# Handing the result rows of routed experts back: scattered by row index or combined on TensorE, with the expert registers read earlier and the residual held in PSUM

## The chip, the cores and the metric

The kernel runs on one core of a Trainium2 chip, in one launch. The metric is the device time of a launch in microseconds (us). In the text and rows, PE is TensorE's matmuls, PEld its weight loads, DVE is VectorE, ACT is ScalarE, POOL is GpSimd and SP is SyncE. All data is float32; matmuls take it either whole (two records for each matmul) or as float32r.

## What is computed

Two layers on x of 2 x 256 tokens with 256 columns: a cross-attention with 16 heads over 512 context rows, and a mixture of experts (32 routed, 4 for each token, one shared), each behind a layer norm and with its residual. The change touches only what follows the attention's last heads.

```python
x = x + _L0_xattn_ref(_layernorm(x, axis=-1), ctx_512, ...)
x = x + _L0_ffn_ref(_layernorm(x, axis=-1), ...)
...
topk_idx, topk_w = _noaux_tc_gate(x, gate_weight, e_score_correction_bias)
combine = jnp.zeros((T, E), x.dtype).at[jnp.arange(T)[:, None], topk_idx].add(topk_w)
def body(acc, packed):
    w1e, w3e, w2e, ce = packed
    return (acc + ce[:, None] * _swiglu(x, w1e, w3e, w2e), None)
routed, _ = lax.scan(body, jnp.zeros_like(x), (w1, w3, w2, combine.T))
shared = _swiglu(x, ws1, ws3, ws2)
return (routed + shared).reshape(b, s, h)
```

T is 512 tokens (four tiles of 128, `TT`), D is 256, E is 32, the hidden width 128.

## The kernel before

Every engine has its own program in `build`, written out by hand in the order in which it runs; semaphores join them. No scheduler is at work.

**End of the attention.** `PLAN` says after which of the 64 score tiles TensorE does which step; `O` steps add a head pair's output projection to `o_ps` (banks 0 and 1). After the last, DVE adds `o_ps` to `x_sb` (L877), takes the statistics and writes the normalised rows `xn`; SP stores them to `xn_rows` in DRAM. TensorE transposes them (`rows_T`) and computes the gate's logits and the shared expert's first layer.

**Routing.** `route`, `slots`, `tables`, `top_weights` and `places` run on DVE. Each expert owns a unit of 128 rows: 64 for the first tokens of that expert and 64 for an overflow block, which may belong to another expert. TensorE turns one-hots into `idx` (L619), a table of the token of each row of each unit, and sums a count into `eo`, the expert of each overflow block. `place` says at which row of `y_rows` a token's four results will lie.

**Registers.** The overflow block's weights are found by a register. L627 reads `eo` with four loads of eight registers and checks each value against its limits. This stands behind the tables and ahead of the unit loop; then TensorE waits for `sh_sum`, DVE's adding of the shared expert (`sy_ps`) to `x_sb` (L1028).

**The unit loop.** POOL gathers a unit's 128 rows (`gather`, L1085) with six buffers: gather u waits until `x_rows(u - 6)` is done. In iteration j TensorE does `x_rows(j)` (transposes, L543), `g_rows(j - 3)` (L561), `hidden(j - 1)` (L552) and `out_rows(j - 3)` (L568). ACT evicts the transposed rows (L747) and does SiLU (L753). DVE multiplies (L1001), evicts the transposed product (L1007) and the result (L1013); SP stores the result to `y_rows` (four buffers, `yu`). Transposed products and results each alternate between two PSUM banks.

**Collection.** When all stores have landed, POOL fetches each token's four result rows, 16 indirect DMAs (`collect`, L1090) of 128 rows; DVE weighs and adds them to `x_sb` (L1041), and SP stores the output.

## Time and profile before

| | us |
|---|---|
| median of 3 runs (362.36 to 362.75) | 362.63 |
| the profiled execution | 362.5 |
| its span, first to last instruction | 360.7 |
| PE / PEld busy in the span | 279.5 / 200.3 |
| DVE / ACT / POOL busy | 230.8 / 171.3 / 138.9 |
| mean granted TensorE clock | 0.914 of 2.4 GHz |

The span is what the trace shows; the profiled execution took 1.8 us more than it. Shares of busy time are an average over a stage that TensorE and DVE share (the attention, to about 227 us), a routing stage where DVE works in short steps, the unit loop (265 to 332 us) where TensorE is busy without a gap, and the collection. The chain of waits, read in order of time, says which engine each moment hangs on; "issue" in it is time for which the profile shows no reason.

### The profile page before, as it was taken

Reading aid. Unit: us, or ns where it says so; the run is one execution under the profiler, and the core shown is the slowest. Engines: PE = TensorE matmul, PEld = TensorE weight load, DVE = VectorE, ACT = ScalarE, POOL = GpSimd, SP = SyncE. Lnnn points to the kernel's source line nnn. Section 1 sums busy time; section 2 is a strip of 40 time slices with the busy share of each in tenths; the row PEclk is TensorE's granted clock in tenths of the full one; section 3 lists DMA queues with packets and bytes.
Section 4 is the critical chain, followed back from the end, with each engine's and each line's share of the span. In section 5 each row is a group of like instructions: output and inputs, shape, how many; then the busy total and the mean of one; then the engine's idle time right before and its main releaser. Section 6 shows DMA issues by size and latency. Waiting matters only on the chain.

```text
span 360.7 us, 5449 instructions
## 1 busy us (share of the span) xinstructions
PE 279.5 (77%) x1662; PEld 200.3 (56%) x1662; DVE 230.8 (64%) x578; ACT 171.3 (47%) x400; POOL 138.9 (39%) x126
## 2 busy tenths in 40 slices
PE   3857869898899998989989898487159999996000
PEld 3634538776587765877758787355125555553000
DVE  4294853889877898968987788668604444443134
ACT  3343745767677786777865565420013333331000
POOL 0641912985009690086910000000544544500672
PEclk9998998999999999999999999968759999999555
DMA  7910015000240001500009957100123444422242
GB/s 253 410 41 0 3 44 190 2 0 0 86 149 3 1 2 26 193 2 0 2 7 351 405 200 253 61 8 1 54 64 105 143 135 139 141 74 85 77 133 85
DMA packets 17595, 35.41 MB, mean 98 GB/s; under 512 B 2848, under 2 KB 10272, under 8 KB 17568
## 3 DMA queue, kind: packets, MB, share of 16 engines
q1 hardware_dynamic: 15264, 28.77, 22.5%
q0 software_dynamic: 2304, 6.29, 6.0%
q8 instruction: 15, 0.25, 0.3%
q14 instruction: 12, 0.10, 0.1%
HBM read 29.81 MB, written 5.24 MB: 97 GB/s over the span
## 4 chain that ended last, share of the span: by engine, by line
PE 48%; DVE 20%; issue 7%; ACT 6%; POOL 4%; DMA 1%; POOLq 0%; ACTq 0%; DVEq 0%
PE bank L552 10%; PE bank L503 6%; PE bank L488 5%; PE bank L568 4%; DVE nmax L828 4%; POOL ctT L1090 4%; PE bank L543 3%; PE bank L465 3%; DVE pT L841 3%; PE bank L443 2%; PE bank L480 2%; PE bank L479 2%; PE bank L413 2%; PE bank L390 2%; PE bank L391 2%
## 5 line engine op out<-in xcount | busy, mean ns | idle before, releaser
L1085 POOL DMA_INDIRECT rope<-xn_rows,idx x32 | 30.4, 951 | 103.5 <-DVE idx L995 74.1
L303 POOL TENSOR_TENSOR rtmp<-abuf,rope 128x512 f32<-128x512 f32 x22 | 29.2, 1325 | 76.9 <-issue 59.6
L828 DVE TENSOR_REDUCE nmax<-bank 128x1 f32<-128x512 f32 x64 | 43.4, 681 | 16.5 <-PE bank L480 15.5
L698 ACT ACTIVATE prob<-bank,nmax 128x512 f32<-128x512 f32 x48 | 33.0, 689 | 30.9 <-DVE nmax L828 30.3
L841 DVE TENSOR_TENSOR pT<-bank,pT 128x512 fp32r<-128x512 f32 x64 | 43.5, 680 | 1.0 <-ACT pT L706 1.0
L706 ACT CAST pT<-bank 128x512 fp32r<-128x512 f32 x64 | 37.6, 590 | 5.6 <-PE bank L488 5.1
L503 PE MATMUL bank<-pT,kvs 128*128 128x256 f32 x256 | 39.0, 296 | 0.6 <-DVE pT L841 0.5
L1001 DVE TENSOR_TENSOR kv<-bank,kv 128x128 f32<-128x128 f32 x32 | 9.3, 291 | 43.3 <-issue 32.7
L552 PE MATMUL bank<-wall,nmat 128*64 (+1 forms) x256 | 36.5, 408 | 0.2 <-ACT nmat L747 0.2
L503 PEld LDWEIGHTS bank<-pT,kvs 128*128 128x128 f32 x256 | 33.1, 193 | 2.0 <-issue 1.0
L488 PE MATMUL bank<-ident,prob 128*128 128x128 f32 x192 | 29.4, 277 | 6.1 <-DVE pT L841 5.4
L488 PEld LDWEIGHTS bank<-ident,prob 128*128 128x128 f32 x192 | 23.0, 142 | 17.6 <-DVE prob L836 9.9
L836 DVE TENSOR_SCALAR prob<-prob,rsum 128x512 f32<-128x512 f32 x48 | 32.5, 677 | 0.1
L747 ACT COPY nmat<-bank 128x256 f32<-128x256 f32 x32 | 11.9, 372 | 39.1 <-PE bank L543 39.1
L306 POOL TENSOR_TENSOR roped<-rtmp 128x512 f32<-128x512 f32 x22 | 29.6, 1347 | 1.7
L304 POOL TENSOR_TENSOR rtmp<-abuf,rope 128x512 f32<-128x512 f32 x22 | 30.3, 1377 | 0.0
L443 PE MATMUL bank<-roped,gmat 128*128 128x512 f32 x48 | 25.4, 638 | 6.1 <-DVE msplit L794 2.8
L479 PE MATMUL bank<-kdup,qsp 128*128 128x512 f32 x64 | 28.1, 439 | 0.8 <-ACT prob L698 0.8
L480 PE MATMUL bank<-kdup,qsp 128*128 128x512 f32 x64 | 25.5, 398 | 0.0
L413 PE MATMUL bank<-wring 128*128 128x192 f32 x64 | 16.6, 400 | 10.8 <-DMA wring<-in_w_attn 4.9
L1090 POOL DMA_INDIRECT ctT<-y_rows,place x16 | 15.1, 946 | 24.2 <-DMA y_rows<-nmat 19.6
L390 PE MATMUL bank<-xnT,msplit 128*128 128x512 f32 x48 | 21.9, 456 | 3.0 <-DVE msplit L794 1.6
(169 smaller groups left out, 527.7 us busy)
## 6 DMA issues: line engine op xcount, KB each, us to landing
wall<-in_w_exp SPq DMA_DIRECT2D x32, 384.0 KB, 7.1
y_rows<-nmat SPq DMA_DIRECT2D x32, 128.0 KB, 1.7
wring<-in_w_attn SPq DMA_DIRECT2D x16, 224.0 KB, 4.1
wring<-in_w_attn SPq DMA_DIRECT2D x4, 640.0 KB, 8.1
wring<-in_w_attn SPq DMA_DIRECT2D x4, 512.0 KB, 7.0
rope<-in_rope_q SPq DMA_DIRECT2D x1, 768.0 KB, 6.7
x_sb<-in_x SPq DMA_DIRECT2D x1, 512.0 KB, 3.5
xn_rows<-xn SPq DMA_DIRECT2D x4, 128.0 KB, 1.8
```

The lines of the kernel that those rows point to most:

```text
L443: mm = pe.matmul(work[u % 2][:, :], gmat[:, j, i, :], roped[:, j, i, :], start=(i == 0), stop=(i == NQT - 1))
L479: pe.matmul(s_ps[t % 3][:, :], q, kdup[:, 0, b * L:(b + 1) * L], start=True, stop=False)
L480: pe.matmul(s_ps[t % 3][:, :], q, kdup[:, 1, b * L:(b + 1) * L], start=False, stop=True) \
L488: mm = pe.transpose(t_ps[t % 2][:, lc * P:(lc + 1) * P], probs[t % 4][:, lc * P:(lc + 1) * P], ident[:, :])
L503: mm = pe.matmul(pv_of(hb), kvs[:, b * LC + lc, :], pT[:, hl, hb % 2, lc, :], start=(n == 0), stop=(n == 2 * LC - 1))
L552: mm = pe.matmul(hu_ps[u % 2][s * BLK:(s + 1) * BLK, 0:2 * I], xTu[:, u % XS, dc, s * BLK:(s + 1) * BLK], wall[:, bass.ds(w + dc * 2 * I, ...
L698: act.activation(probs[t % 4], s_ps[t % 3][:, :], ACT.Exp, bias=nmax[:, t:t + 1], accum_out=psum_e[:, t:t + 1]).then_inc(s_exp, 1)
L706: act.copy(pT[:, 0, hb % 2, :, (t % 2) * P:(t % 2 + 1) * P], t_ps[t % 2][:, :].rearrange("p (c q) -> p c q", c=LC)).then_inc(t_hi, 1)
L828: dve.tensor_reduce(nmax[:, t:t + 1], s_ps[t % 3][:, :], AX.X, ALU.max, negate=True).then_inc(s_max, 1)
L836: dve.tensor_scalar(probs[t % 4], probs[t % 4], rsum[:, t:t + 1], None, ALU.mult).then_inc(s_norm, 1)
L841: dve.tensor_tensor(pT[:, 1, hb % 2, :, q], t_ps[t % 2][:, :].rearrange("p (c q) -> p c q", c=LC), f(pT[:, 0, hb % 2, :, q]), ALU.subtract ...
L1085: pool.indirect_dma_start(xg[:, u % XG, :], None, xn_dram, bass.IndirectOffsetOnAxis(idx[:, 1, u:u + 1], 0)) \
```

## The change

**Units in two kinds.** Twenty units are SENT: ACT evicts the result times the row's weight (`wslot`), and POOL scatters its 128 rows (`scatter`) to `y_rows`, which is now laid out by rank and token; rows without a token go to a region behind. Twelve are DIRECT (4, 9, 14, 19 and 24 to 31): ACT writes the weighted result as float32r (`y_hi`), DVE the rest (`y_lo`), DVE compares the unit's token indices with an iota row (`choose`), and TensorE adds one-hot times result into `sy_ps`, the shared expert's accumulators, eight float32r matmuls a unit (`combine`). A token's ranks that no scatter wrote have to read as zero, so SP fills 2 MB of `y_rows` with zeros early on. The collection is four plain loads on SP of a token's four ranks, summed on DVE in iterations j = 31 to 34 (`sum_rows`); the last four additions take `sy_ps`.

**Weights by slot.** `places` goes; `slot_weights` makes two more one-hot tables on DVE, and TensorE turns them into `wslot` at j = 1.

**Banks.** Transposed products have one bank and results have one (5), since bank 2 and now 7 hold `sy_ps`.

**Registers.** They are read before the tables, without the limit checks, and `eo` is made earlier in `slots`. `d_ws`, the weights' semaphore, is waited for ahead of the loop.

**x in PSUM.** Step `S0` at tile 62 adds x to `o_ps` by an identity matmul. Statistics and normalisation read PSUM; ACT copies the sum to `x_sb` beside the gate. The addition of the shared expert before the loop goes.

```diff
+DIRECT = (4, 9, 14, 19) + tuple(range(24, NU))
+SENT = tuple(u for u in range(NU) if u not in DIRECT)
+SUMS = {28: 0, 29: 1, 30: 2, 31: 3}
...
-        yu_ps = (bank[2], bank[5])
+        gt_ps = bank[6]
+        yu_ps = bank[5]
...
-            {0: "-N0", 1: "-N1", 3: "O0 O1", 5: "O2 O3", 8: "O4", 10: "O5", 12: "O6"},
+            {0: "-N0", 1: "-N1", 3: "O0 O1", 5: "O2 O3", 8: "O4", 10: "O5", 12: "O6", 14: "S0"},
...
+            sp.wait_ge(zero_set, 1)
+            sp.dma_start(y_dram[0:TOPK * T, :].rearrange("(p a r) d -> p a (r d)", p=P, a=TOPK * T * D // (P * T)),
+                         ctT[:, NP - 1, :].unsqueeze(1).to_broadcast([P, TOPK * T * D // (P * T), T])).then_inc(d_zero, 16)
...
-            for u in range(NU):
-                sp.wait_ge(yu_ev, u + 1)
-                sp.dma_start(y_dram[u * P:(u + 1) * P, :], yu[:, u % YS, :]).then_inc(d_yu[u % YS], 16)
+            for r in range(YS):
+                sp.wait_ge(d_yu[r], 16 * len(SENT[r::YS]))
+            for tt in range(TT):
+                sp.dma_start(y4[:, tt, :, :], y_dram[0:TOPK * T, :].rearrange("(k t p) d -> t p k d", k=TOPK, t=TT)[tt]) \
+                    .then_inc(d_y4[tt], 16)
...
+                elif kind == "S":
+                    for tt in range(TT):
+                        pe.matmul(o_ps[tt // 2][:, (tt % 2) * D:(tt % 2 + 1) * D], ident[:, :], x_sb[:, tt, :],
+                                  start=False, stop=False, skip_group_check=True)
...
+                if u >= 1 and u - 1 in SENT:
+                    pe.wait_ge(yu_ev, SENT.index(u - 1) + 1)
+                elif u >= 1:
+                    pe.wait_ge(y_low, DIRECT.index(u - 1) + 1)
                 for s, w in enumerate((over_w[u], u * WE)):
-                    pe.matmul(yu_ps[u % 2][s * BLK:(s + 1) * BLK, 0:D], gTu[:, u % GS, s * BLK:(s + 1) * BLK],
+                    pe.matmul(yu_ps[s * BLK:(s + 1) * BLK, 0:D], gTu[:, u % GS, s * BLK:(s + 1) * BLK],
                               wall[:, bass.ds(w + 2 * ND * I, D)], start=True, stop=True).then_inc(yu_mm, 1)
+
+            def combine(u):
+                n = DIRECT.index(u)
+                pe.wait_ge(picked, n + 1)
+                pe.wait_ge(y_low, n + 1)
+                for tt in range(TT):
+                    for k, part in enumerate((y_hi, y_lo)):
+                        mm = pe.matmul(sy_ps[tt // 2][:, (tt % 2) * D:(tt % 2 + 1) * D], pickc[:, n % 2, tt * P:(tt + 1) * P],
+                                       part[:, n % 2, :], start=False, stop=(u == DIRECT[-1] and k == 1), skip_group_check=True)
+                    if tt % 2 == 1 and (u == DIRECT[-1] or tt == TT - 1):
+                        mm.then_inc(comb_mm, 1)
...
+            pe.wait_ge(eo_done, 1)
+            over_w = []
+            for u in range(0, NU, 8):
+                _, regs = nc.values_load_multi_w_load_instructions(
+                    eo[0:1, u:u + 8], [mybir.EngineType.PE], min_val=0, max_val=(E - 1) * WE,
+                    skip_runtime_bounds_check_because="VectorE takes the minimum with the last expert just before")
+                over_w.extend(regs)
...
             pe.wait_ge(d_ws, 16 * E)
-            pe.wait_ge(eo_done, 1)
-            over_w = []
-            for u in range(0, NU, 8):
-                _, regs = nc.values_load_multi_w_load_instructions(eo[0:1, u:u + 8], [mybir.EngineType.PE], min_val=0,
-                                                                   max_val=(E - 1) * WE)
-                over_w.extend(regs)
-            pe.wait_ge(sh_sum, TT)
-            for j in range(NU + 3):
+            for j in range(NU + 4):
                 if j < NU:
                     x_rows(j)
-                if j >= 3:
+                if 3 <= j < NU + 3:
                     g_rows(j - 3)
+                if j - 4 in DIRECT:
+                    combine(j - 4)
                 if 1 <= j <= NU:
                     hidden(j - 1)
-                if j >= 3:
+                if 3 <= j < NU + 3:
                     out_rows(j - 3)
+                if j == 1:
+                    pe.wait_ge(one_w_done, 1)
+                    for k in range(NK):
+                        for s in range(2):
+                            mm = pe.matmul(invw_ps[s * BLK:(s + 1) * BLK, :], one_r[:, k, :],
+                                           one_w[:, s * T + k * E:s * T + (k + 1) * E], start=(k == 0), stop=(k == NK - 1))
+                            if k == NK - 1:
+                                mm.then_inc(invw_mm, 1)
...
+            def y_evict(u):
+                act.wait_ge(yu_mm, 2 * u + 2)
+                if u in SENT:
+                    n = SENT.index(u)
+                    if n >= YS:
+                        act.wait_ge(d_yu[n % YS], 16 * (n // YS))
+                    act.activation(yu[:, n % YS, :], yu_ps[:, 0:D], ACT.Copy, scale=wslot[:, u:u + 1]).then_inc(yu_ev, 1)
+                else:
+                    n = DIRECT.index(u)
+                    if n >= 2:
+                        act.wait_ge(comb_mm, n - 1)
+                    act.activation(y_hi[:, n % 2, :], yu_ps[:, 0:D], ACT.Copy, scale=wslot[:, u:u + 1]).then_inc(y_top, 1)
+
+            for j in range(NU + 3):
                 if j < NU:
                     x_evict(j)
-                if j >= 1:
+                if 1 <= j <= NU:
                     silu(j - 1)
+                if j == 3:
+                    act.wait_ge(w_done, 1)
+                if j >= 3:
+                    y_evict(j - 3)
...
-                dve.tensor_tensor(x_sb[:, tt, :], o_ps[tt // 2][:, (tt % 2) * D:(tt % 2 + 1) * D], x_sb[:, tt, :],
-                                  ALU.add).then_inc(x1_done, 1)
-                if tt >= 1:
-                    dve.wait_ge(x1_done, tt)
-                    dve.bn_stats(stat[:, TT + tt - 1, :], x_sb[:, tt - 1, :]).then_inc(x1_stat, 1)
-            dve.wait_ge(x1_done, TT)
-            dve.bn_stats(stat[:, 2 * TT - 1, :], x_sb[:, TT - 1, :]).then_inc(x1_stat, 1)
+                dve.bn_stats(stat[:, TT + tt, :], x1(tt)).then_inc(x1_stat, 1)
...
+            def slot_weights():
+
+                top = topw[:, 1, :, :].rearrange("p t k -> p (t k)")
+                link(dve.scalar_tensor_tensor(wvals[:, :], pick[:, :], 4096.0, top, ALU.is_ge, ALU.mult))
+                dve.tensor_tensor(one_w[:, 0:T].rearrange("p (i e) -> p i e", e=E), sel_a.rearrange("p (i e) -> p i e", e=E),
+                                  top.unsqueeze(2).to_broadcast([P, NK, E]), ALU.mult)
+                dve.tensor_tensor(one_w[:, T:2 * T].rearrange("p (i e) -> p i e", e=E), eq_v.rearrange("p (i e) -> p i e", e=E),
+                                  wvals[:, :].unsqueeze(2).to_broadcast([P, NK, E]), ALU.mult).then_inc(one_w_done, 1)
+                dve.wait_ge(invw_mm, 2)
+                dve.tensor_copy(wslot[:, :], invw_ps).then_inc(w_done, 1)
...
+            def choose(u):
+                n = DIRECT.index(u)
+                if n >= 2:
+                    dve.wait_ge(comb_mm, n - 1)
+                dve.tensor_scalar(pickc[:, n % 2, :], iota_t, tokf[:, u:u + 1], None, ALU.is_equal).then_inc(picked, 1)
+
+            def y_rest(u):
+                n = DIRECT.index(u)
+                dve.wait_ge(y_top, n + 1)
+                dve.scalar_tensor_tensor(y_lo[:, n % 2, :], yu_ps[:, 0:D], wslot[:, u:u + 1], f(y_hi[:, n % 2, :]),
+                                         ALU.mult, ALU.subtract).then_inc(y_low, 1)
+
+            def sum_rows(tt):
+                dve.wait_ge(d_y4[tt], 16)
+                two = pair.rearrange("p (k d) -> p k d", k=2)
+                link(dve.tensor_tensor(two, y4[:, tt, 0:2, :], y4[:, tt, 2:4, :], ALU.add))
+                link(dve.tensor_tensor(x_sb[:, tt, :], two[:, 0, :], x_sb[:, tt, :], ALU.add))
+                link(dve.tensor_tensor(x_sb[:, tt, :], two[:, 1, :], x_sb[:, tt, :], ALU.add))
...
             for j in range(1, NU + 3):
+                if j - 3 in DIRECT:
+                    choose(j - 3)
                 if j >= 3:
                     gT_evict(j - 3)
                 if j <= NU:
                     gated(j - 1)
-                if j >= 3:
-                    y_evict(j - 3)
-            dve.wait_ge(sh_sum, TT)
+                if j - 3 in DIRECT:
+                    y_rest(j - 3)
+                if j - 3 in SUMS:
+                    sum_rows(SUMS[j - 3])
             for tt in range(TT):
-                dve.wait_ge(d_y4[tt], 16 * TOPK)
-                for k in range(TOPK):
-                    last = dve.scalar_tensor_tensor(x_sb[:, tt, :], y4[:, tt, k, :], topw[:, 1, tt, k:k + 1], x_sb[:, tt, :],
-                                                    ALU.mult, ALU.add)
-                    if k < TOPK - 1:
-                        link(last)
-                last.then_inc(fin, 1)
+                dve.wait_ge(comb_mm, len(DIRECT) + tt // 2)
+                dve.tensor_tensor(x_sb[:, tt, :], sy_ps[tt // 2][:, (tt % 2) * D:(tt % 2 + 1) * D], x_sb[:, tt, :],
+                                  ALU.add).then_inc(fin, 1)
...
-            def collect(tt, k):
-                i = tt * TOPK + k
-                pool.indirect_dma_start(y4[:, tt, k, :], None, y_dram, bass.IndirectOffsetOnAxis(place[:, 1, i:i + 1], 0)) \
-                    .then_inc(d_y4[tt], 16)
+            def scatter(u, n):
+                pool.wait_ge(yu_ev, n + 1)
+                pool.indirect_dma_start(y_dram, bass.IndirectOffsetOnAxis(idx[:, 0, u:u + 1], 0), yu[:, n % YS, :], None) \
+                    .then_inc(d_yu[n % YS], 16)
 
             for tt in range(TT):
                 pool.wait_ge(d_xn[tt], 16)
             pool.wait_ge(idx_done, 1)
             for u in range(XG):
                 gather(u)
-            for u in range(XG, NU):
-                gather(u)
-            pool.wait_ge(placed, 1)
-            for r in range(YS):
-                pool.wait_ge(d_yu[r], 16 * (NU // YS))
-            for tt in range(TT):
-                for k in range(TOPK):
-                    collect(tt, k)
+            pool.wait_ge(d_zero, 16)
+            for u in range(NU):
+                if u in SENT:
+                    scatter(u, SENT.index(u))
+                if u + XG < NU:
+                    gather(u + XG)
```

On TensorE, before, the end of the register reading (the last of four loads, each with 16 checking instructions, ISA) stood right ahead of the first `x_rows` (L543) and behind the one-hot matmuls of the tables (L619):

```order
L627 TENSOR_LOAD eo
L627 ISA x16
L543 MATMUL bank3<-ident,rope 128x128 [waits d_xg0,sh_sum]
L543 MATMUL bank3<-ident,rope 128x128
L543 MATMUL bank4<-ident,rope 128x128 [waits d_xg1]
```

Now the four loads stand between the shared expert's last matmuls (L645, `rtmp` holding its weights) and those one-hot matmuls (L662):

```order
L645 MATMUL bank7<-rtmp,prob 128x256 x2
L651 TENSOR_LOAD eo [waits eo_done]
L651 TENSOR_LOAD eo x3
L662 MATMUL bank5<-ctT 64x32 [waits r_done,st_done,ov_one]
L662 MATMUL bank5<-ctT 64x32 x7
```

The loads went ahead of the tables, and the checks are gone.

On POOL, in the unit loop and the collection, there stood before (`rope` holds gathered rows, `nmat` the result buffers, `ctT` the collected rows):

```order
L1085 DMA rope<-xn_rows,idx 128x256 [waits d_xn2,d_xn3,d_xn1,idx_done,d_xn0,rope_p]
L1085 DMA rope<-xn_rows,idx 128x256 x5
L1085 DMA rope<-xn_rows,idx 128x256 [waits xt_mm] x26
L1090 DMA ctT<-y_rows,place 128x256 [waits d_yu2,d_yu1,d_yu3,d_yu0,placed]
L1090 DMA ctT<-y_rows,place 128x256 x15
```

And now the first rows of the loop are:

```order
L1166 DMA rope<-xn_rows,idx 128x256 x5
L1171 DMA y_rows<-nmat,idx 6144x256 [waits yu_ev,d_zero]
L1166 DMA rope<-xn_rows,idx 128x256 [waits xt_mm]
L1171 DMA y_rows<-nmat,idx 6144x256 [waits yu_ev]
L1166 DMA rope<-xn_rows,idx 128x256 [waits xt_mm]
```

A scatter stands between two gathers, and the collection is gone from POOL.

On TensorE, in the iteration of unit 24 and those after it, before (L561 `g_rows`, L552 `hidden`, L568 `out_rows`):

```order
L561 MATMUL bank7<-ident,kv 128x128 [waits gt_ev,gu_done]
L552 ISA [waits gu_done,xt_ev]
L552 MATMUL bank1<-wall,nmat 64x256 x2
L552 ISA
L552 MATMUL bank1<-wall,nmat 64x256 x2
L568 ISA [waits yu_ev,gt_ev]
L568 MATMUL bank5<-wall,ctmp 64x256 x2
```

and now, `kdup` holding one-hots and the two parts of the result:

```order
L586 MATMUL bank6<-ident,kv 128x128 [waits gt_ev,gu_done]
L604 MATMUL bank2<-kdup 128x256 [waits y_low,picked]
L604 MATMUL bank2<-kdup 128x256 x3
L604 MATMUL bank7<-kdup 128x256 x4
L577 ISA [waits gu_done,xt_ev]
L577 MATMUL bank0<-wall,nmat 64x256 x2
L577 ISA
L577 MATMUL bank0<-wall,nmat 64x256 x2
L595 ISA [waits y_low,gt_ev]
L595 MATMUL bank5<-wall,ctmp 64x256 x2
```

`combine` of a unit comes between `g_rows` and `hidden`, and `out_rows` waits for the low part of the unit before.

## Rows read from the trace of the kernel before

**Rows 1.** Chain of waits before the unit loop: start us, us, what.
```profile
259.89 5.62 issue
...
266.64 0.13 issue
266.77 1.98 PE bank L552 x8
```

**Rows 2.** Timeline of POOL and DVE: start, us, engine line op names, idle before.
```profile
255.53 1.15 POOL L1085 DMA_INDIRECT rope<-xn_rows,idx  x1 [74.11 <-DVE idx L995]
...
273.48 0.41 DVE L1013 COPY nmat<-bank 128x256 f32<-128x256 f32 x1
...
273.96 0.94 POOL L1085 DMA_INDIRECT rope<-xn_rows,idx  x1 [0.98 <-PE bank L543]
```

**Rows 3.** Chain of waits in the unit loop.
```profile
273.69 0.11 PE bank L561
...
325.33 0.37 PE bank L543 x2
...
325.81 1.01 PE bank L552 x8
326.83 0.43 PE bank L568 x4
```

**Rows 4.** Chain of waits in the collection.
```profile
332.09 0.43 DVE nmat L1013
332.54 1.68 DMA y_rows<-nmat
...
334.99 0.94 POOL ctT L1090
335.93 0.30 issue
...
353.74 2.76 DMA ctT<-y_rows,place
...
358.09 0.48 DVE x_sb L1041
```

**Rows 5.** Timeline of TensorE: shared expert's last layer, then the slot tables.
```profile
247.39 3.60 PE L607 MATMUL bank<-rtmp,prob 128*128 128x256 f32 x8
...
251.92 2.06 PE L619 MATMUL bank<-ctT 128*64 128x32 f32 x64 [0.93 <-DVE ctT L973]
```

**Rows 6.** Chain of waits from the last score tiles to the statistics.
```profile
208.58 1.73 PE bank L465 x8
...
211.65 0.95 PE bank L503 x8
...
222.32 0.14 issue
...
224.45 0.04 issue
...
227.86 0.75 DVE x_sb L877 x2
...
230.59 0.29 DVE mv L886 x4
```

**Rows 7.** Windows before the loop: stretch, length, engines' busy us, PEclk, DMA, GB/s.
```profile
256.00:257.00 1.00, 0.00 (x0) 0.00 (x0) 0.89 (x4) 0.00 (x0) 0.69 (x2) 1.00 0.00 0
258.00:259.00 1.00, 0.00 (x0) 0.00 (x0) 0.93 (x5) 0.00 (x0) 0.77 (x1) 0.50 0.32 82
```

**Rows 8.** One window of the attention, same columns.
```profile
27.00:36.00 9.00, 6.94 (x22) 4.08 (x21) 4.13 (x7) 3.25 (x7) 1.38 (x2) 0.88 0.00 0
```

**Rows 9.** Instructions of L1085 and L836: ns minimum/median/maximum.
```profile
L1085 POOL DMA_INDIRECT rope<-xn_rows,idx x32: 940/944/1147, 255.5 to 314.4; - x32
L836 DVE TENSOR_SCALAR prob<-prob,rsum x48: 468/478/1392, 36.4 to 220.0; 128x512 f32<-128x512 f32 x48
```

**Rows 10.** DMA issues on the page: KB each, us to landing.
```profile
x_sb<-in_x SPq DMA_DIRECT2D x1, 512.0 KB, 3.5
```

99 lines of the change are left out of this document (51 added, 48 removed).

## The prediction

> **What bounds the kernel now.** I read the chain of waits first, then timelines of its stages. From 251.92 TensorE runs the 32 small matmuls of the slot tables (64 records, 2.06 us), and after some DVE work the chain has 5.62 us of "issue" before the first `x_rows` at 265.51 [rows 1, 5]. TensorE had ended those matmuls at 253.98 [rows 5]: it is idle for 11.5 us while its sequencer loads 32 registers and checks them (L627). The rows of unit 0 had been on their way since 255.53 [rows 2], so the registers end this wait, not the gather. Then the unit loop is pure TensorE: 0.37 + 0.11 + 1.01 + 0.43 = 1.93 us a unit (the rows round), with nothing between [rows 3]. DVE, ACT and POOL have room; POOL waits 0.98 us before each gather and is busy 0.95 [rows 2]. After the last eviction at 332.52 comes the collection: 1.68 us for the last store, then 16 indirect DMAs on POOL, each 0.95 busy and 0.30 apart, the last landing 2.76 after its start, and the last adds, to 358.57 [rows 4]. The profiled execution took 362.5 us for a span of 360.7, 1.8 us beyond it; the median is 362.63. I add 1.8 to a span. One indirect DMA costs POOL 1.25 us, and that number carries this forecast.
>
> **Start of the loop.** The loads move to between the shared expert's last matmuls (end 250.99 [rows 5]) and the slot tables, whose inputs are ready at 251.9; the new `eo` step ahead of `pick` makes that 252.0. They lose 64 checking instructions. No row shows one load. Bounds: 0 (all 11.5 us were the checks) and 11.5 (all were the loads). A checking instruction resembles the register step that stands ahead of a matmul. With one, the matmul starts 0.13 us after its releaser (266.64 to 266.77 [rows 1]); the shortest start without one is 0.04 (224.45 to 224.49 [rows 6]). That is at most some 0.08 us each, 5.1 for 64, and leaves 11.5 - 5.1 = 6.4 us for the four loads. I take 6.4. TensorE then starts the tables at 251.0 + 6.4 = 257.4. The clock was at 1.00 (2.4 GHz) in the slice up to 257 and at 0.50 (1.2 GHz) in the one after 258, TensorE idle since 253.98 [rows 7]; now it is idle from 251.0, so the 2.06 us of small matmuls run at half, 4.1 us, to 261.5. Index arithmetic and POOL's start take 1.55 (253.98 to 255.53), the first gather 1.15 [rows 2], and the row block lands about 1.85 after that (2.76 less 0.95 [rows 4]). First `x_rows`: 266.05 instead of 265.51. Moving the loads thus puts them in front of tables and gather, which used to be ahead of them: no gain.
>
> The Trainium skill prices the loads in two ways. "Runtime: NRT & Kernel Launch", section "Instruction fetch mechanics", gives about 200 ns for a register, by which estimate 32 take 6.4 us. "DMA: Bandwidth & Descriptors", section "Latency and other measured facts", gives a floor of about 600 ns for a `tensor_load`; by that estimate four take 2.4 us, and the kernel would come out near 364.
>
> **x in PSUM.** Step S0 adds four matmuls of the form of L465, 1.73 us, before `transposes(62)`; about 0.7 of it falls into waits that TensorE has there for `pT` (one of 0.14 stands in the chain at 222.32 [rows 6]), so +1.0. The four additions (0.37 each at the first pair's rate) leave the chain from 227.86 to 230.88 [rows 6], -1.4; reading PSUM in the normalisation may give 0.1 back. Net -0.3, which I set to zero; bounds -1.4 and +0.5. The two ACT copies of x lie beside TensorE's `logits`, before whose end ACT has nothing to do. The zero fill of 2 MB is queued behind the constants at about 15 us and can run when the queues are empty (the slice from 27 to 36 moved 0 GB/s [rows 8]). Zero. The removed `places` and x sums on DVE lay beside the register loads: zero.
>
> **Until the first scatter.** Before, unit 0 is evicted at 273.89, 8.4 us after the first `x_rows` [rows 2]. New on TensorE is the weight table at j = 1, another 64 records, 2.06 to 4.1 us, partly in the loop's first stretch at the half clock (1.98 for the L552 group there, 1.01 later [rows 1, 3]); its inputs are ready 4.2 us after the indices, so it does not wait. With 0.27 us until POOL starts after a release (273.69 to 273.96 [rows 2, 3]), scatter 0 begins 11.0 us after the loop: 277.1. POOL idles before it, since gather 6 stands behind it.
>
> **The scattered stretch.** POOL now does a scatter and a gather for each sent unit: 2 x 1.25 = 2.5 us against TensorE's 1.93. A scatter is not in the trace; I price it as a gather of the same 128 rows (bounds 0.94 and 1.15 busy, the extremes of L1085 [rows 9]). TensorE waits for the gather. Where a direct unit comes (4, 9, 14, 19), POOL saves a scatter, but the next scatter must wait for TensorE. The loop closes like this: scatter 5, +2.5, scatter 6, +2.5, scatter 7, +1.25, gather 13 starts, +2.85, it has landed and `x_rows(13)` starts, +3.03 (0.37 + 0.11 + about 0.1 waiting + 0.95 combining unit 9 + 1.01 + 0.43 + 0.05), +0.71 (ACT's eviction with scale, 0.40, near DVE's 0.43 for the same size [rows 4], a hand-over and POOL's 0.27), scatter 10. Sum 12.83 us for five units, where TensorE alone took 5 x 1.93 = 9.64. The 0.95 is L503's chain share, the same form (f32r, 128x256, eight of them) [rows 6].
> From scatter 0: scatter 5 at 289.9 (scatter 2 at 282.1, then 1.25 + 2.85 + 3.03 + 0.71), scatter 20 after three turns at 328.4, scatter 22 at 333.4, gather 28 landed and `x_rows(28)` at 337.5. Before it was at 319.55 (325.33 less three units [rows 3]): the loop is 18 us late.
>
> **The combined stretch.** POOL has done its last gathers. With one PSUM bank for results, `combine(u)` and `out_rows(u+1)` wait for both readers of unit u: from the end of `out_rows` ACT's high part, 0.4, DVE's low part, 0.45 (L1013's 0.43, L1041's 0.48 [rows 4]), and the hand-overs, 1.13 in all. Then 0.95 + 1.01 + 0.43: 3.52 us a unit instead of 1.93. `x_rows(31)`: 337.5 + 2.94 + 2 x 3.52 = 347.5; `out_rows(28)` ends at 351.1. The last three go by DVE: low part (1.0 after `out_rows`), `sum_rows` 1.5 (L877's 0.37 [rows 6] twice for its 128x512 and once for each of two more), `choose` 0.48 (L836's median [rows 9]), the transposed eviction 0.29 (within the gap of a unit), hand-over 0.13, `out_rows` 0.43: 3.83 each, 362.6. Then 0.93 to the low part, 1.45 for the last `sum_rows`, which hides the last combination, four additions of 0.37: 366.4. The store and the end take 2.1 (358.57 to 360.7): span 368.5, time 370.4.
> What hides the four big loads of `y4`: scatter 23 lands at 338.7, and a 512 KB load took 3.5 us [rows 10], so even one after the other they land by 352.7, each before its `sum_rows` (352 and later).
>
> So the collection, 26 us from 332.5, is gone, but the loop grows by 18 us and its end, from `x_rows(31)` at 325.3 in the old kernel and 347.5 in the new, still takes 19 us to the last addition. Sum: +0.5 start, +2.6 weight table and POOL's start, +14.8 POOL's pace, +4.2 for units 28 to 31, -14.3 at the end (33.2 becomes 18.9): +7.8.
>
> A rule that would add to this: "SBUF — State Buffer" of the Trainium skill, in its part on the shared port pair, says that a DVE copy or `tensor_scalar` in a two-port mode keeps GpSimd from writing descriptors until it ends. In the trace L836, such an operation, takes 0.47 us at least and 1.39 at most beside POOL's multiplications [rows 9], so the two do exclude each other. `choose` is of that form; by the rule the four in POOL's stretch could add up to 0.5 each, 2 us, near 372.
>
> **Rivals.**
> A. The loads cost next to nothing; the 11.5 us were the checks. Then the tables run at 252.0 at the full clock, indices are ready at 254.8, `x_rows(0)` at 258.6, everything 7.5 us earlier: 362.9. For it: 64 checks against 4 loads. Against it: a register step ahead of a matmul costs under 0.1.
> B. The side of a gain: as A, and TensorE's clock stays up, because it idles only 4.6 us before the loop (it still had 1.00 in the slice up to 257 [rows 7]). By the L552 groups, the loop's start at half (1.98) costs 2.2 us more than at full (1.01) over its first two units and the weight table: 360.7, faster. It decides from where the loads take under 1 us; above that the clock has fallen.
> C. Scatters cost POOL more than gathers, as the first gather did (1.15) or more by the time that their target rows take: 20 x 0.2 to 0.5 = 4 to 10 us less what hides: 374 to 379.
> D. POOL's 0.30 pause is not paid between unlike DMAs: a pace of 1.05 gives 366.5.
>
> **How the numbers follow.** Forecast with its bounds (364 to 373, the loads between 2.4 and 8 us) and D: 0.57. A: 0.14. B, with a cheaper POOL beside A: 0.18. C: 0.11. The likeliest is 370.4. The range leaves out C's upper part and what lies under B: 360.7 to 376. Faster by over 0.2% (below 361.9) is B: 0.18; within 0.2%, about what a measurement can tell, is over half of A: 0.08; slower: 0.74.
>
> **What would show it.** Right: `x_rows(0)` near 266; scatters 2.5 us apart with TensorE waiting for `rope` in the loop; 12.8 us for five units; `x_rows(28)` near 337; 3.5 us a unit afterwards. The register step is wrong if the tables start before 254. POOL's step is wrong if a scatter is busy for other than 0.95 us or follows by other than 0.30. The end is wrong if `sum_rows` waits for `y4`. Above all the forecast falls if the first `x_rows` comes before 260 and POOL's pace is under 1.2 us.

## The result and the profile after

The changed kernel takes 383.49 us (382.16 to 386.39, four runs) where the kernel before took 362.5 in the same runs: a ratio of 1.060 (95% interval 1.053 to 1.067). The prediction said 370.4, with a range up to 376.0: the direction is right, the size is 13 us short. The profiled execution has a span of 381.2, against a forecast of 368.5. Some kernels below have executions a few per cent longer than their fastest, and the profiles of direct_seventh, scatter_pause, scatter_two and scatter_shuffled are of such executions: of these four I use the times and the pattern, and not the span of the profile.

The head of the page (busy time, then slices of 9.5 us with TensorE's granted clock) and the two groups of POOL's DMAs on it:

```profile
span 381.2 us, 5736 instructions
...
PE 305.1 (80%) x1830; PEld 219.4 (58%) x1830; DVE 229.1 (60%) x561; ACT 183.7 (48%) x434; POOL 144.6 (38%) x130
...
PEclk9999999998999999999999985965999698999985
...
L1166 POOL DMA_INDIRECT rope<-xn_rows,idx x32 | 31.4, 983 | 87.0 <-DVE idx L1054 77.6
...
L1171 POOL DMA_INDIRECT y_rows<-nmat,idx x20 | 19.8, 989 | 34.5 <-ACT nmat L810 31.7
```

A scatter keeps POOL busy for 0.99 us, 0.05 more than a gather in [rows 2]; as an instruction it was priced well. But POOL, which the forecast made the bound, waits 31.7 us for ACT's eviction. And the clock, besides the 5 at the loop's start (the slice at 257), drops to 6 once more in the loop, in the slice at 295.

The start of the loop (timeline: start, us, engine, line, operation, in brackets the idle time before it and what ended it), to set beside [rows 2, 5]:

```profile
244.92 1.99 PE L645 MATMUL bank<-rtmp,prob 128*128 128x256 f32 x8
...
249.54 3.10 PE L662 MATMUL bank<-ctT 128*64 128x32 f32 x64 [2.62 <-DVE ctT L1046]
...
254.16 1.15 POOL L1166 DMA_INDIRECT rope<-xn_rows,idx  x1 [77.59 <-DVE idx L1054]
...
257.30 0.66 PE L568 MATMUL bank<-ident,rope 128*128 128x128 f32 x2 [4.66 <-DMA rope<-xn_rows,idx]
```

The register loads stand between the first two rows. TensorE was idle for 2.62 us there, and what ended it was VectorE's one-hots. The first `x_rows` comes at 257.30, 8.7 us earlier than forecast. Traces of the runs below with the same program up to that point have it between 257.30 and 262.24, so a difference of a few us there, from one trace to another, says little.

Now the place where the time goes: units 7 to 9 of the sent stretch, timeline of all engines.

```profile
287.69 0.99 POOL L1171 DMA_INDIRECT y_rows<-nmat,idx  x1 [0.30 <-issue]
...
288.98 0.97 POOL L1166 DMA_INDIRECT rope<-xn_rows,idx  x1 [0.30 <-issue]
...
289.62 1.08 PE L577 MATMUL bank<-wall,nmat 128*64 x8
...
290.25 0.99 POOL L1171 DMA_INDIRECT y_rows<-nmat,idx  x1 [0.30 <-issue]
290.54 0.60 PE L595 MATMUL bank<-wall,ctmp 128*64 x4
291.55 0.97 POOL L1166 DMA_INDIRECT rope<-xn_rows,idx  x1 [0.30 <-issue]
291.70 0.44 PE L568 MATMUL bank<-ident,rope 128*128 128x128 f32 x2 [0.56 <-DMA rope<-xn_rows,idx]
291.98 0.27 PE L586 MATMUL bank<-ident,kv 128*128 128x128 f32 x1
292.18 1.08 PE L577 MATMUL bank<-wall,nmat 128*64 x8
293.73 0.28 ACT L802 ACTIVATE kv<-bank 128x128 f32<-128x128 f32 x1 [3.73 <-PE bank L577]
293.90 0.47 ACT L810 ACTIVATE nmat<-bank,wslot 128x256 f32<-128x256 f32 x1
294.04 0.29 DVE L1073 TENSOR_TENSOR kv<-bank,kv 128x128 f32<-128x128 f32 x1 [4.02 <-ACT kv L802]
...
294.26 0.37 ACT L796 COPY nmat<-bank 128x256 f32<-128x256 f32 x1
294.51 0.30 ACT L802 ACTIVATE kv<-bank 128x128 f32<-128x128 f32 x1
294.64 0.28 DVE L1079 COPY ctmp<-bank 128x128 f32<-128x128 f32 x1
294.65 0.99 POOL L1171 DMA_INDIRECT y_rows<-nmat,idx  x1 [2.13 <-ACT nmat L810]
...
295.07 1.12 PE L595 MATMUL bank<-wall,ctmp 128*64 x4 [1.80 <-DVE ctmp L1079]
```

`hidden` (L577) began at 289.62 and lasts 1.08, so ACT's SiLU (L802) was due just after 290.7; it starts at 293.73. Meanwhile TensorE goes on: `out_rows` (L595), the next `x_rows` (L568), `g_rows` (L586) and `hidden`. Within a microsecond ACT and VectorE then do what waited for all of these, five steps in a row with hardly a pause: TensorE's work was finished, as far as the modelled ends of matmuls tell, and only the news of it came late. The trace bears this out: it also has the time of each semaphore update, which the views do not print. The `hidden` that ended at 290.71 has its updates at 293.00 and 293.71, `out_rows` (291.14) at 293.75 and 293.79, `x_rows` (292.14) at 293.84 and `g_rows` (292.25) at 293.87; TensorE's updates otherwise follow an end by 0.01 us (median). Updates of the DMA of the scatter begun at 290.25 stand at 292.50, in the midst of it. I call this a **late signal**; the expectations below also call it a burst, since the signals that were held come all at once. TensorE itself, waiting in turn, gets behind: `out_rows` at 295.07 already runs at the half clock (1.12 instead of 0.60). The same picture stands ahead of units 14, 19 and 24, a smaller one ahead of unit 4, each time after the third of three scatters in a row (the fourth sent unit of each run of four is itself held). A row of ACT's waits from 270 to 335 sums it up (us in total, times, longest):

```profile
ACT kv L802 <- PE bank L577: 25.9, 14, 4.2
```

Such a row also counts waits for a TensorE that is itself slow: with a combined unit they are 2.67, and more at the half clock. The time from the end of `hidden` to ACT's SiLU on it is the sharper measure. It is 0.07 us in most units of every run, and over 2 us in four units here (2.99 to 3.04).

A turn of five units takes 17.3 us (`x_rows(10)` at 286.14, `x_rows(20)` at 320.66) instead of the forecast 12.8. The combined stretch is near its forecast, 3.84 us a unit instead of 3.52:

```profile
357.30 0.60 PE L595 MATMUL bank<-wall,ctmp 128*64 x4
...
357.98 0.47 ACT L815 ACTIVATE kdup<-bank,wslot 128x256 fp32r<-128x256 f32 x1 [0.15 <-PE bank L595]
...
358.48 0.48 DVE L1090 SCALAR_TENSOR_TENSOR kdup<-bank,wslot,kdup 128x256 fp32r<-128x256 f32 x1 [0.34 <-ACT kdup L815]
...
359.12 1.18 PE L604 MATMUL bank<-kdup 128*128 128x256 f32 x8 [0.73 <-DVE kdup L1090]
...
360.23 1.08 PE L577 MATMUL bank<-wall,nmat 128*64 x8
361.14 0.60 PE L595 MATMUL bank<-wall,ctmp 128*64 x4
```

### The profile page after: what moved, and what is told of

Same layout as the page of the kernel before. It is cut to its first block, busy times and chain, and to the rows that moved or that the text cites. A ratio compares the mean times of both kernels' runs of the same rounds, so it can differ in the third digit from the quotient of the medians.

```text
span 381.2 us, 5736 instructions
## 1 busy us (share of the span) xinstructions
PE 305.1 (80%) x1830; PEld 219.4 (58%) x1830; DVE 229.1 (60%) x561; ACT 183.7 (48%) x434; POOL 144.6 (38%) x130
## 4 chain that ended last, share of the span: by engine, by line
PE 46%; DVE 19%; ACT 8%; issue 6%; DMA 4%; POOL 3%; another core or an unknown queue 2%; DVEq 0%; ACTq 0%; POOLq 0%
PE bank L528 6%; PE bank L577 6%; PE bank L513 5%; PE bank L485 4%; DMA rope<-xn_rows,idx 4%; PE bank L595 3%; DVE nmax L895 3%; PE bank L604 3%; PE bank L463 2%; DVE pT L908 2%; PE bank L505 2%; PE bank L504 2%; POOL y_rows L1171 2%; PE bank L410 2%
## 5 line engine op out<-in xcount | busy, mean ns | idle before, releaser
L1166 POOL DMA_INDIRECT rope<-xn_rows,idx x32 | 31.4, 983 | 87.0 <-DVE idx L1054 77.6
L577 PE MATMUL bank<-wall,nmat 128*64 (+1 forms) x256 | 38.3, 424 | 0.0
L802 ACT ACTIVATE kv<-bank 128x128 f32<-128x128 f32 x32 | 9.0, 280 | 55.4 <-PE bank L577 47.4
L1171 POOL DMA_INDIRECT y_rows<-nmat,idx x20 | 19.8, 989 | 34.5 <-ACT nmat L810 31.7
L463 PE MATMUL bank<-roped,gmat 128*128 128x512 f32 x48 | 23.7, 599 | 6.1 <-DVE msplit L861 2.8
L595 PE MATMUL bank<-wall,ctmp 128*64 (+1 forms) x128 | 21.2, 412 | 9.0 <-DVE ctmp L1079 7.8
L568 PE MATMUL bank<-ident,rope 128*128 128x128 f32 x64 | 15.2, 322 | 14.2 <-DMA rope<-xn_rows,idx 12.5
```

What stands on the lines that cost most here:

```text
L577: mm = pe.matmul(hu_ps[u % 2][s * BLK:(s + 1) * BLK, 0:2 * I], xTu[:, u % XS, dc, s * BLK:(s + 1) * BLK], wall[:, bass.ds(w + dc * 2 * I, ...
L595: pe.matmul(yu_ps[s * BLK:(s + 1) * BLK, 0:D], gTu[:, u % GS, s * BLK:(s + 1) * BLK], wall[:, bass.ds(w + 2 * ND * I, D)], start=True, sto ...
L1166: pool.indirect_dma_start(xg[:, u % XG, :], None, xn_dram, bass.IndirectOffsetOnAxis(idx[:, 1, u:u + 1], 0)) \
```

## The experiments: what holds the start of the loop

All runs are set against runs of the kernel before beside them, where its median was 361 to 363 us.

**unchecked_late**: the kernel before, with the bounds checks of the loads left out.

```
-                _, regs = nc.values_load_multi_w_load_instructions(eo[0:1, u:u + 8], [mybir.EngineType.PE], min_val=0,
-                                                                   max_val=(E - 1) * WE)
+                _, regs = nc.values_load_multi_w_load_instructions(
+                    eo[0:1, u:u + 8], [mybir.EngineType.PE], min_val=0, max_val=(E - 1) * WE,
+                    skip_runtime_bounds_check_because="VectorE takes the minimum with the last expert just before")
```

> The kernel before with the bounds checks of the four register loads left out, and the loads where they were. The prediction split TensorE's 11.5 us of idle ahead of x_rows(0) into 5.1 for the 64 checks and 6.4 for the loads: by that x_rows(0) comes 5.1 us earlier, near 260.4. If the checks are the whole of it and the loads next to nothing, x_rows(0) comes near 259.9, where regs_early has it and where the last addition of the shared result ends. If the checks are nothing and the position of the loads all, it stays at 265.5.

Measured: 357.87 (357.71 to 358.02), ratio 0.989 (0.984 to 0.993). The first `x_rows` of its timeline:

```profile
260.35 1.11 PE L543 MATMUL bank<-ident,rope 128*128 128x128 f32 x4 [5.95 <-DVE x_sb L1029]
```

The wait now ends with VectorE's last addition of the shared result, and the loads fit into 5.95 us unseen. The run does not tell the prediction's split (260.4 expected) from checks alone (259.9).

**regs_early**: the same, and the loads moved ahead of the tables as in the change (the step that makes `eo` ahead of `pick`).

> The kernel before with one edit: the four register loads stand where the changed kernel has them (behind the shared expert's result, ahead of the tables) and carry no bounds check. If the loads and checks were what TensorE waited for between its tables and x_rows(0) (11.5 us of idle in the kernel before), x_rows(0) comes near 258.5 and the time falls by 6 to 8 us, to 355 to 357. If something else fills that wait (gathers landing, the shared additions), x_rows(0) stays after 263 and the gain is under 2.5 us.

Measured: 358.33 (357.83 to 360.12), ratio 0.990 (0.986 to 0.993); `x_rows(0)` at 259.86. The start came as expected, but only 4 us of the 6 to 8 arrive. A part goes at once: the gathers run without a pause up to unit 8, and ACT's waits from 258 to 275 hold one that the view can put down to no instruction:

```profile
ACT kv L754 <- remote: 2.4, 1, 2.4
```

A late signal, then (`hidden` ended at 266.92, SiLU began at 269.59), with no scatter in the program; it did not come back in unchecked_late or in best0 (below), whose gathers run without a pause for as long.

**checks_back**: the changed kernel with the checks put back (the edit above, reversed).

> The changed kernel with the bounds checks of the register loads put back, the loads early as they are. The shared expert's result ends at 246.9 and the tables began at 249.5. The prediction had 6.4 for the loads and 5.1 for the 64 checks: by that the loads alone would have put the tables at 253.3, and with checks they begin at 258.4 (246.9 and 11.5). Since the loads hid in 2.6 us of wait, the checks must be 8.9 or more of the 11.5 if the idle was theirs: again 258.4, and x_rows(0) near 266. If the tables begin before 254, the 11.5 us of the kernel before were mostly something else than loads and checks (the additions until 259.9, say). Time 386 to 392 if 258.4, 383 to 386 if earlier.

Measured: 393.86 (391.47 to 396.26), 10.4 us slower than the changed kernel and 1.9 over the range that I gave it.

```profile
246.46 3.78 PE L645 MATMUL bank<-rtmp,prob 128*128 128x256 f32 x8
259.65 3.63 PE L661 MATMUL bank<-ctT 128*64 128x32 f32 x64 [9.41 <-issue]
...
267.88 0.66 PE L568 MATMUL bank<-ident,rope 128*128 128x128 f32 x2 [4.60 <-DMA rope<-xn_rows,idx]
```

TensorE is idle for 9.41 us for loads and checks, 2.1 less than the 11.5 of the same instructions in the kernel before. What hid the rest no row shows, since the loads have no record; `eo` was ready at 247.31, beside L645, and I take it that the sequencer began them there. So the bounds have to allow for that. In the changed kernel `eo` was ready at 245.83 and the tables began at 249.54: the loads take at most 3.71 us. In the kernel before, loads and checks take at least 11.5. That leaves at least 7.8 us for the 64 checks, 0.12 each, and not the 0.08 at most that I had allowed.

## The experiments: the late signals

Theory 1: they come from what POOL's queue does (six indirect DMAs in a row, three of them scatters). Theory 2: they come with the combined units, since they fall just ahead of them.

**plain_send**: the scatters leave POOL; SP stores the rows to places of their own, and the output lacks the sent part.

```
-                if u in SENT:
-                    scatter(u, SENT.index(u))
...
+            for n, u in enumerate(SENT):
+                sp.wait_ge(yu_ev, n + 1)
+                sp.dma_start(y_dram[(TOPK * TT + u) * P:(TOPK * TT + u + 1) * P, :], yu[:, n % YS, :]).then_inc(d_yu[n % YS], 16)
```

> The changed kernel, but the 20 sent units' rows go by plain stores on SP's queue to rows of their own, and POOL issues gathers alone; the sent rows are not placed by token, so their part of the sum is left out. Theory 1 (in the changed kernel TensorE's completion signals come out up to 3 us late each time POOL has issued six indirect DMAs back to back): the five late bursts of signals vanish, five-unit cycles take under 12 us instead of 15.3 to 17.6, and the time falls by 18 us or more, to 365 or less. Theory 2 (the late signals come from the combined units' instructions, which fall in the same places): the bursts stay before units 4, 9, 14, 19 and 24, and the time falls by 8 us or less.

Measured: 363.68 (362.98 to 365.89), 19.8 under the changed kernel. A turn of five units takes 11.5, and ACT's longest wait for `hidden` is that of a combined unit:

```profile
ACT kv L805 <- PE bank L580: 21.7, 14, 2.7
```

**direct_third** and **direct_seventh** move the combined units:

```
-DIRECT = (4, 9, 14, 19) + tuple(range(24, NU))
+DIRECT = (2, 5, 8, 11, 14, 17, 20, 23) + tuple(range(24, NU))
```

```
-DIRECT = (4, 9, 14, 19) + tuple(range(24, NU))
+DIRECT = (6, 13, 20) + tuple(range(24, NU))
```

> The changed kernel with units 2, 5, 8, 11, 14, 17, 20, 23 and 24 to 31 combined on TensorE: two sent units between combined ones, so that POOL has five indirect DMAs in a row (6.4 us) where three units of TensorE take 7.5. Theory 1 (late signals come from POOL's unbroken run of six): no late bursts, four more combined units cost TensorE about 1.6 each (6.5), five bursts of 2.5 to 3 us are saved (12 to 14), the time is 374 to 379. Theory 2 (they come with the combined units): eight bursts before unit 24 instead of four or five, the time is 393 or more.

> The changed kernel with units 6, 13, 20 and 24 to 31 combined: six sent units between combined ones, so that POOL has longer runs. Theory 1 (late signals come with POOL's sixth DMA in a row): more than one burst in each stretch of six sent units, some of them three units away from any combined one; about 6 to 8 bursts, the time is 385 to 392. Theory 2 (they come with the combined units): three or four bursts, each just before units 6, 13, 20 and 24, the time is 378 to 382.

Measured: direct_third 380.12 (376.56 to 386.44), direct_seventh 389.48 (381.89 to 391.37). In direct_third, with runs of two scatters, waits of over 3 us are rare (two, at 338.5 and 343.6, against six in the changed kernel), and one SiLU starts over 2 us after its `hidden` (3.18, at 338.52, two scatters and three gathers without a pause before it). But POOL's pace keeps the gain small, and the time is a little over theory 1's. The time of direct_seventh does not decide: three executions lie in theory 1's range (388 to 391), one, of 381.89, in theory 2's. The trace does: one of the late signals stands in the middle of a run of sent units, three units from any combined one, right after the third scatter without a pause (291.90, 294.48, 297.05):

```profile
297.05 0.99 POOL L1171 DMA_INDIRECT y_rows<-nmat,idx  x1 [0.30 <-issue]
...
299.03 1.08 PE L577 MATMUL bank<-wall,nmat 128*64 x8
300.41 0.28 ACT L802 ACTIVATE kv<-bank 128x128 f32<-128x128 f32 x1 [3.61 <-PE bank L577]
```

Theory 2 falls. The count of bursts that I expected of theory 1 (six to eight) did not come either: in four units SiLU came over 2 us late (2.5 to 3.7). POOL had gone idle after the held units, so runs without a pause stayed at about three scatters.

What is it about POOL's queue? Four runs put something else where the scatter stood; the output lacks the sent part in each.

**dummy_gathers**: stores as in plain_send, and on POOL an indirect gather of as many rows into a scratch tile.

```
+                    pool.indirect_dma_start(dum[:, n % 2, :], None, xn_dram, bass.IndirectOffsetOnAxis(idx[:, 1, u:u + 1], 0)) \
+                        .then_inc(d_dum[n % 2], 16)
```

> The kernel of the run plain_send (plain stores on SP's queue in place of the scatters; the sent part of the sum is left out), with one thing put back on POOL: where a scatter stood, POOL waits as before for the evicted rows and issues an indirect gather of as many rows into a scratch tile that nobody reads. Theory 1a (TensorE's signals come late when POOL issues indirect DMAs without a pause, whichever way they move data): the late bursts come back, about one for each three sent units, and the time is 376 to 386. Theory 1b (only the scattered writes do it): no bursts, POOL's pace alone costs, five-unit cycles of 12.8 us, the time is 366 to 374.

**pool_work**: the same with an addition of 128x384 on POOL in the place of the DMA.

> The same, but POOL runs an addition of about 1 us where a scatter stood, and no DMA. Theory 1a: what matters is the issue of DMAs, so the late bursts stay away; POOL is as busy as with scatters, and the time is 364 to 374. Rival (it is enough that POOL is busy beside TensorE): the bursts come back and the time is over 376.

**pool_store**: POOL's queue writes the tile, but in one plain store.

```
-                pool.indirect_dma_start(y_dram, bass.IndirectOffsetOnAxis(idx[:, 0, u:u + 1], 0), yu[:, n % YS, :], None) \
+                pool.dma_start(y_dram[(TOPK * TT + u) * P:(TOPK * TT + u + 1) * P, :], yu[:, n % YS, :]) \
```

> The changed kernel with one word of each scatter changed: POOL's queue still writes the 20 sent tiles to DRAM, but in plain stores to rows of their own and not by an index (the sent part of the sum is left out). If any write that POOL issues holds TensorE's signals back, the late bursts stay and the time is over 376. If it takes the indexed write, there are no bursts and the time is 364 to 371, near that of plain_send (363.7) and of dummy_gathers (370.9).

**scatter_in_row**: the scatter as it is, its indices made consecutive.

```
+                dve.tensor_scalar(idx[:, 0, :], pad_row, -1.0, None, ALU.add)
```

> The changed kernel, but the scatters' indices are consecutive rows of each unit's own (the sent part of the sum is left out): the same instructions on POOL, the same bytes, only the place of the rows in DRAM is in order. If the rows' places matter, no late bursts of signals and 366 to 373, as with gathers in the scatters' place (370.9). If it is the indexed write itself, the bursts stay (after the third scatter in a row) and the time is 380 to 386.

Measured: dummy_gathers 370.88 (367.63 to 374.12), pool_work 367.24 (365.91 to 368.58), pool_store 367.20 (366.18 to 368.22), scatter_in_row 372.10 (371.75 to 372.44). From 270 to 335 none has a wait of ACT for `hidden` beyond 2.7 us. From scatter_in_row:

```profile
ACT kv L802 <- PE bank L577: 23.2, 24, 2.2
```

The third scatter of a run in scatter_in_row, and the rows behind it, to set beside the 287 to 295 of the changed kernel:

```profile
290.23 1.08 PE L577 MATMUL bank<-wall,nmat 128*64 x8
...
290.84 0.99 POOL L1172 DMA_INDIRECT y_rows<-nmat,idx  x1 [0.30 <-issue]
...
291.39 0.28 ACT L802 ACTIVATE kv<-bank 128x128 f32<-128x128 f32 x1 [0.79 <-PE bank L577]
```

So neither a busy POOL, nor DMAs without a pause, nor writes from POOL's queue, nor the scatter instruction does it by itself. Theory 1a falls as well. What scatter_in_row changed was where the rows go: to neighbouring rows, in another part of DRAM. One run parts these two.

**scatter_shuffled**: scatter_in_row with a fixed permutation of the 4096 rows of the same part of DRAM.

```
-    moe_c[:, C_PAD:C_VAL] = TOPK * T + 1 + np.arange(NU) * P + row
+    perm = np.random.RandomState(1).permutation(NU * P).reshape(P, NU)
+    moe_c[:, C_PAD:C_VAL] = TOPK * T + 1 + perm
```

> The run scatter_in_row with its indices put through one fixed permutation of all 4096 rows of the same part of DRAM (again the sent part of the sum is left out; the gathers of unused slots read other rows than before, which changes no count of them). If the order of the rows in DRAM is what holds TensorE's signals, the late bursts are back after the third scatter in a row and the time is 378 to 386. If it is the part of DRAM (the changed kernel's first 2048 rows), there are none and the time is 369 to 374.

Measured: 385.52 (382.22 to 388.82), 10 to 17 us above scatter_in_row (two executions each), with the late signals in the changed kernel's place and size, again after the third scatter:

```profile
299.32 0.99 POOL L1172 DMA_INDIRECT y_rows<-nmat,idx  x1 [0.31 <-issue]
...
302.68 0.28 ACT L802 ACTIVATE kv<-bank 128x128 f32<-128x128 f32 x1 [3.60 <-PE bank L577]
```

It is where the written rows lie to each other. (The permutation also changes which rows the gathers read for unused slots; those of the changed kernel are as in scatter_in_row, so that isn't it.) "Order" below stands for two things that no run parts: a unit's 128 rows are in another order, and they are spread over 4 MB in place of 128 KB side by side. A shuffle within each unit's own rows was not run. How many scatters it takes, and how dense:

**scatter_half**: every second sent unit scattered, the others stored by SP. **scatter_two**: the third of each four sent units goes by SP. Both outputs lack what SP stores. **scatter_pause**: the whole changed kernel, with an addition of 1 us on POOL ahead of the third scatter of each four.

Of the first, and of the second:

```
-                if u in SENT:
+                if u in SENT and SENT.index(u) % 2 == 0:
```

```
-                if u in SENT:
+                if u in SENT and SENT.index(u) % 4 != 2:
```

> The changed kernel with every second sent unit scattered by POOL and the others stored plainly on SP's queue (their part of the sum is left out): ten scatters, never two in neighbouring sent units. If the late signals belong to each scatter alone, about half of the loss stays: 371 to 376, with late bursts. If they need scatters one behind the other (the third of a run of three, as in the changed kernel and in direct_seventh), there are none, POOL keeps pace, and the time is 363 to 367.

> The changed kernel with the third sent unit of each run of three stored plainly by SP (its part of the sum is left out), so that no more than two scatters follow each other; 15 scatters in all. If it takes three in a row, no bursts and 368 to 373 (five DMAs fewer on POOL than in dummy_gathers' 370.9). If every pair of scatters does some of it, 374 to 381.

> The changed kernel, whole, with an addition of about 1 us on POOL ahead of every third scatter of a run of three (five of them in all). If what matters is how densely the DMAs follow each other, the pause costs 5 x 1.3 = 6.5 on POOL and takes the bursts away (5 x 2.3): 376 to 380. If it is the number of scatters in a run whatever the spacing, the bursts stay and the time is 384 to 390.

Measured: scatter_half 370.61 (369.80 to 371.42), scatter_two 372.14 (368.86 to 375.43), scatter_pause 377.05 (373.38 to 380.72). The first two have no wait of ACT for `hidden` over 3 us in the loop, scatter_pause two, just over 3. scatter_half is slower than the 363 to 367 that I expected if scatters do nothing alone: a turn takes 14 us, with waits for gathers, and why it isn't 12.5 I did not settle. scatter_pause says that the density counts: each pause moves POOL's third scatter by 0.9 us (4.5 for five, where I had allowed 6.5), and the kernel is still some 6 faster. Its two executions lie 7 us apart, so the size is rough.

The sharper measure, from the end of `hidden` to its SiLU, parts the runs cleanly, and the waits just over 3 us in scatter_pause turn out to be waits for TensorE's work and not late signals:

| run | units over 0.2 us | over 2 us | longest, us |
|---|---|---|---|
| changed kernel | 13 | 4 | 3.04 |
| checks_back | 13 | 4 | 2.94 |
| scatter_shuffled | 10 | 4 | 3.90 |
| direct_seventh | 9 | 4 | 3.72 |
| direct_third | 12 | 1 | 3.18 |
| regs_early | 3 | 1 | 2.67 |
| the other 13 runs and the kernel before | 0 | 0 | 0.08 |

## The experiments: a version that beats both

If scattered writes are what is dear, and the collection at the end was what the change set out to remove, the two can be parted: store plainly, and collect while the last units are combined on TensorE.

**best0** is the kernel before with the early unchecked loads, x in PSUM, and the four shared additions ahead of the weights on VectorE.

> The kernel before with its own loop, stores and collection, and three edits: the register loads as in the run regs_early; x kept in PSUM through the second norm as in the changed kernel; the four additions of the shared expert's result moved ahead of the weights and places on VectorE, so that they no longer hold the first x_rows. If the changed kernel's earlier start (about 2 us by x in PSUM) is real, and the additions held x_rows(0) in regs_early until 259.9, x_rows(0) comes near 256 and the time falls 2 to 4 us under regs_early's 358.3, to 354.5 to 356.5. If the start of the loop is held by the gathers and late signals instead, the gain over regs_early is under 1 us.

Measured: 355.57 (354.63 to 356.55), ratio 0.984 (0.980 to 0.988); `x_rows(0)` at 257.38. So x in PSUM and the moved additions bring some 2 to 3 us over regs_early (2.8 by the times, 2.1 by the ratios); in the traces 1.5 us of the difference lie behind `x_rows(0)`, where regs_early had its late signal. How the rest divides is not shown.

**late_combined** is the changed kernel with units 24 to 31 combined, plain stores for the rest, and the collection of the kernel before, with the rows of combined units pointing at zeros:

```
-DIRECT = (4, 9, 14, 19) + tuple(range(24, NU))
+DIRECT = tuple(range(24, NU))
...
+                link(dve.tensor_scalar(placef[:, 0, :], placef[:, 1, :], float(P * DIRECT[0]), None, ALU.is_lt))
+                dve.scalar_tensor_tensor(place[:, 1, :], placef[:, 1, :], float(P), placef[:, 0, :], ALU.add, ALU.mult).then_inc(placed, 1)
```

> The changed kernel with only units 24 to 31 combined on TensorE; the rows of the other 24 go by plain stores on SP's queue, and POOL collects them with 16 indirect gathers while the last eight units run (rows of combined units point at a row of zeros). The loop then has POOL at one DMA per 1.93 us. From the rows: 24 units at 1.93 (46.3), eight at 3.8 (30.4), some 8 us of last unit and last additions, from x_rows(0) near 257.5: 342 to 346 at the end of the span, a time of 344 to 348, if the collection is covered. If TensorE's signals are held through the 16 gathers in a row, up to 20 us come back and the time is 355 to 366.

Measured: 353.81 (352.26 to 356.84), ratio 0.977 (0.972 to 0.982). The 16 gathers of the collection ran without a pause beside TensorE and held no signal. The time is 6 over the top of what I expected: the start of the loop took 13.5 us for five units because of the weights' table, the whole profile was 4 us late already at `x_rows(0)` (261.75), and each of the last units carried VectorE's additions in its chain.

**tuned7** (units 25 to 31 combined) and **tuned8** (24 to 31) remove that; against late_combined:

```
             slots()
-            tables()
             top_weights()
+            slot_values()
+            tables()
...
-                if j - 4 in DIRECT:
-                    combine(j - 4)
                 if 1 <= j <= NU:
                     hidden(j - 1)
+                if j - 4 in DIRECT:
+                    combine(j - 4)
...
+                    if j - 2 < NU:
+                        choose(j - 2)
+                        gT_evict(j - 2)
                     y_rest(j - 3)
```

> The run late_combined with four edits: seven combined units (25 to 31); VectorE makes the weights and their one-hots ahead of its wait for the first tables, and TensorE builds the table of weights right behind the first tables, while it waits for the first gather anyway; combine stands behind hidden on TensorE; on VectorE choose and gT_evict of the next unit stand ahead of y_rest. Expected from late_combined's rows: 3 to 4 us at the start of the loop (x_rows(0) to x_rows(5) took 13.5 there, 10.1 in best0), 0.2 a combined unit, 1.9 for the unit that is no longer combined, and 0.5 to 1.5 for each of the last three units: 345 to 349 in all. If the collection's end sets the end (it starts 1.9 us later), 349 to 352.

> The run tuned7 with unit 24 combined as well: the collection starts 1.93 us earlier, TensorE does 1.3 more (3.23 a combined unit against 1.93). In tuned7 the last collected tile was waited for 2.4 us (340.60) while TensorE had ended at 337.9. If the end is set by the later of the two, it comes 1 us earlier (346 to 348 us of time); if TensorE's end decides, it is 0.5 to 1.3 later (348 to 350).

Measured: tuned7 348.12 (347.02 to 349.23), ratio 0.962 (0.958 to 0.966); tuned8 346.17 (345.68 to 347.52), ratio 0.958 (0.952 to 0.964). TensorE makes the table of weights while it waits for the first gather, and the last wait before the first `x_rows` is 0.17:

```profile
254.82 3.63 PE L670 MATMUL bank<-rtmp,ctT 128*64 128x32 f32 x64 [1.61 <-DVE idx L1068]
...
258.61 0.66 PE L568 MATMUL bank<-ident,rope 128*128 128x128 f32 x2 [0.17 <-DMA rope<-xn_rows,idx]
```

A combined unit takes 3.23 us, and the end is TensorE's and VectorE's, with no wait for the collection left:

```profile
336.81 1.19 PE L604 MATMUL bank<-kdup 128*128 128x256 f32 x8 [1.28 <-DVE kdup L1107]
...
339.87 1.42 DVE L1149 TENSOR_TENSOR x_sb<-bank,x_sb 128x256 f32<-128x256 f32 x4
```

Part of the gain over the kernel before is that of best0's edits, which these two have as well (the loads early and without checks, x in PSUM, no additions ahead of the loop). Against best0, tuned8 is 9.4 us faster (355.57 less 346.17).

## Why the prediction was right and wrong

**The register loads: wrong.** The step that failed is "a checking instruction resembles the register step that stands ahead of a matmul", at most 0.08 us each, which left 6.4 us to the loads. Measured: loads at most 3.71, checks at least 7.8. The tables began at 249.54, not 257.4, and by the prediction's own sign ("wrong if the tables start before 254") the step was wrong at a glance. Rival A was right on the loads; with 0.14 it had too little. Rival B, the same with the clock staying up, was not: TensorE idled for 4.66 us ahead of `x_rows(0)`, and the granted clock from 257 to 260 was 0.50. The row I compared with was a register step with nothing behind it; 64 of another kind were not in the trace, and both ends of the bound (0 and 11.5) were equally open. The Trainium skill's two figures divide in the same way: its "Runtime: NRT & Kernel Launch", section "Instruction fetch mechanics", has about 200 ns a register, for loads that the page describes as from HBM. These came from SBUF, and the trace contradicts the figure for them (32 in at most 3.71 us, 116 ns each at most). The Trainium skill's "DMA: Bandwidth & Descriptors", section "Latency and other measured facts", has a floor of 600 ns a `tensor_load`, and by that estimate four of these, 2.4 us, would fit under 3.71.

**x in PSUM: not shown to be wrong.** I set it to zero between -1.4 and +0.5. best0's tables start 0.6 earlier than regs_early's (249.60 against 250.24), which differs from it up to there by this part alone. But unchecked_late and the kernel before, the same program up to there, differ by 0.4 at the last one-hots (251.78 against 251.36), so the runs say only that the effect is small.

**Until the first scatter: short by 2.1.** It took 13.1 us from `x_rows(0)` (257.30 to 270.42) and not 11.0: POOL started 0.8 us after the eviction instead of 0.27, and the weights' table ran 3.58 at the half clock (0.50 from 258 to 264).

**POOL's pace: nearly right, but not the bound.** The forecast was 12.83 us for five units, and the changed kernel took 17.3. dummy_gathers, which has POOL's DMAs but no scattered writes, turns in 13.2, scatter_in_row in 13.3. Busy 0.99 and pause 0.30 are as forecast. The failed step is "a scatter is not in the trace; I price it as a gather of the same 128 rows". As an instruction that holds; its effect on TensorE's signals was outside what the row of a gather could show. From scatter 0 to `x_rows(28)` the kernel took 75.1 us and the forecast 60.4; scatter_in_row took 63.6. So 11.5 of the 14.7 are the order of the rows, the rest pace. By the medians (383.5 less 372.1) it is 11.4. This term, the wait for TensorE's signals, was not in the prediction at all. Rival C named the target rows, but as POOL's time, with 374 to 379 for it. The half clock after two of the four late signals is a part of it: from 294 to 302 the granted clock was 0.57, from 311 to 318 0.79, but 1.00 from 328 to 335 and from 343 to 349. In scatter_in_row it was 1.00 from 294 to 302 (windows: length, busy time and count of the five engines, clock, DMA share, GB/s; first the changed kernel):

```profile
294.00:302.00 8.00, 6.56 (x29) 4.03 (x30) 2.04 (x7) 1.98 (x8) 2.90 (x3) 0.57 0.16 49
```

```profile
294.00:302.00 8.00, 7.28 (x57) 4.26 (x53) 2.31 (x8) 3.36 (x10) 4.89 (x6) 1.00 0.27 83
```

**The combined stretch: short by 0.3 a unit.** The mechanism is as described (one bank, two readers); the terms are 1.22, 1.11, 0.91 and 0.60 instead of 1.13, 0.95, 1.01 and 0.43. The last units took 4.1 to 4.6 instead of 3.83, the last of them at the half clock. That `y4` is not waited for was right, though its loads took 7.2 us and not 3.5. From `x_rows(31)` to the end it was 23.4 instead of 21.0.

**The sum.** Start -8.7, first units +2.1, sent stretch +14.7, units 28 to 31 +2.3, end +2.4: 12.7 (the parts are rounded), which is 381.2 against 368.5. Without the scattered order the two main errors would nearly have cancelled: scatter_in_row's 372.1 lies 1.7 from the forecast, for the wrong reason.

**The port rule.** The prediction cited that by the Trainium skill's "SBUF — State Buffer", in its part on the shared port pair, `choose` could hold POOL by up to 0.5 us. The one gather of the changed kernel that began beside a `choose` in POOL's stretch took 1.20 instead of 0.97, so 0.2 is lost; the other three times POOL was idle. The one case agrees with the rule, and its price here is next to nothing.

## What to carry to other kernels

Price an instruction that the trace does not have by what it does to memory and to its neighbours, too, not only by the busy time of its nearest relative: here twenty scatters cost 10 us or more by where their rows lay, and their rows in order cost no more than gathers in their place (372.1 and 370.9). Where rows must change their order, store them in order and gather them out of order, and put that gathering beside work that does not need it (346 us here, against 383 with scatters and 356 for best0, whose gathers stand alone at the end). Leave out runtime checks on registers by an argument in the code before you think about moving the loads.

## What the runs showed of the hardware

- TensorE's completions can reach ACT and VectorE up to 3.9 us late while TensorE works on. It came after three indirect scatters to rows out of order, 2.6 us apart, in the changed kernel, direct_seventh, scatter_shuffled and checks_back; once with two in a row (direct_third); not in the traces with a pause of 1 us (scatter_pause) or with the third stored (scatter_two), nor with rows in order (scatter_in_row), plain stores or gathers in the loop. One case at a loop's start (regs_early) had gathers only. What in the chip holds them is open: these runs vary what POOL sends, and the trace has only the time at which an update took effect.
- Whether the taking of the trace has a part in it is open too. The six traces with late signals lack 15 to 23% of their DMAs' semaphore records (446 of 2112 in the changed kernel, none in scatter_in_row). But the kernel before lacks 13% and plain_send 7%, without a late signal.
- The scatter's time on POOL did not depend on the order (0.99 us in both).
- A runtime bounds check on a register costs TensorE at least 0.12 us; 32 register loads from SBUF fit into 3.7 us.
- Sixteen indirect gathers without a pause, beside TensorE's combined units, cost it nothing (late_combined).
